# A smaller first batch, and its first expert phase run beside the routing of the last six tiles

## The reference

```python
h = tok(x, W, b); h = concatenate([cls_tok, h], axis=1)
h = h + attn(layernorm(h))                       # 12 heads; a neighbour filter on the scores before the softmax
# the experts, on y = layernorm(h):
logits_fk = (y @ W_fk + b_fk) @ normed(emb_fk).T   # 128 experts, first layer
logits_rk = (y @ W_rk + b_rk) @ normed(emb_rk).T   # 128 experts, second layer
w_fk = top4_of_softmax(logits_fk); w_rk = top4_of_softmax(logits_rk)
mid = sum_n w_fk[n] * (y   @ f_know[n])            # f_know: 128 matrices of 192 x 128
out = sum_n w_rk[n] * (mid @ r_know[n])            # r_know: 128 matrices of 128 x 192
h = h + out
```

## Time and profile before

| | us |
|---|---|
| runs (median of three) | 835.84, 830.92, 826.09 (830.92) |
| profiled execution | 832.31 |
| its span | 830.6 |
| groups 5 and 6 on PE | 240.9 to 280.5, 280.5 to 322.2 |
| last matmul of the attention groups | 346.6 |
| phase 0, first transpose to `experts_done[0]` | 408.3 to about 491 |
| phase 1, first transpose to last matmul | 491.5 to 577.6 |
| phase 2 | 629.0 to 698.9 |
| phase 3 | 713.1 to 775.6 |

### The profile page before, as it was taken

The page is one execution under the profiler, slowest core; times in us unless marked ns, Lnnn a source line. Parts: engine busy times, 40 slices in busy tenths (PEclk is TensorE's granted clock), DMA queues, the critical chain, the costliest instruction groups (busy, mean ns, idle before and its releaser), DMA issues.

```text
span 830.6 us, 16386 instructions
## 1 busy us (share of the span) xinstructions
PE 565.4 (68%) x5060; PEld 456.6 (55%) x5061; DVE 382.3 (46%) x1355; ACT 340.8 (41%) x738; POOL 403.8 (49%) x397
## 2 busy tenths in 40 slices
PE   6898998989999947516698859865018775777200
PEld 6686876868787836303578746654015453546100
DVE  2836678878676888998860001111111110133132
ACT  4337385564757425223255524432002553244100
POOL 2432260532514040767374027777667771576374
PEclk9689999999897968556699977988558998897755
DMA  5896769587840743395388747869996886588532
GB/s 138 315 364 275 262 239 386 206 346 279 325 170 21 156 98 77 106 284 139 107 270 238 203 119 202 234 187 293 309 291 187 266 264 185 169 242 255 171 99 69
DMA packets 151442, 177.44 MB, mean 214 GB/s; under 512 B 12777, under 2 KB 134930, under 8 KB 151378
## 3 DMA queue, kind: packets, MB, share of 16 engines
q1 hardware_dynamic: 138002, 149.20, 56.8%
q0 software_dynamic: 13376, 27.41, 11.6%
HBM read 76.55 MB, written 100.02 MB: 213 GB/s over the span
## 4 chain that ended last, share of the span: by engine, by line
PE 32%; DVE 19%; issue 12%; DMA 12%; POOL 11%; ACT 9%; SPq 4%; POOLq 0%; ACTq 0%; DVEq 0%
POOL gat L703 7%; PE bank L845 7%; DMA xs<-mid_dram 6%; PE bank L1133 4%; ACT qk_pad L1223 4%; PE bank L892 3%; POOL mid_dram L711 3%; PE bank L1107 3%; PE bank L1122 3%; DVE pick L1832 3%; DMA gat<-wide_dram,slots 3%; PE bank L1140 2%; PE bank L830 2%; SPq L494 2%; DVE smax L1609 2%
## 5 line engine op out<-in xcount | busy, mean ns | idle before, releaser
L703 POOL DMA_INDIRECT gat<-wide_dram,slots x152 | 145.7, 959 | 128.5 <-SPq L539 76.7
L1107 PE MATMUL bank<-ident,xs 128*96 128x128 f32 (+1 forms) x480 | 91.8, 305 | 62.7 <-DMA xs<-mid_dram 22.8
L1391 ACT ACTIVATE xsT<-bank 96x512 f32<-96x512 f32 (+1 forms) x160 | 76.4, 487 | 121.3 <-PE bank L1107 117.8
L1382 ACT ACTIVATE os<-bank 128x256 f32<-128x256 f32 (+1 forms) x160 | 70.1, 438 | 116.5 <-PE bank L1133 68.0
L647 POOL TENSOR_TENSOR qk_sum<-qk_pad 64x888 f32<-64x888 f32 x16 | 26.6, 1664 | 179.2 <-ACT qk_pad L1223 165.6
L1107 PEld LDWEIGHTS bank<-ident,xs 128*96 128x96 f32 (+1 forms) x480 | 59.4, 165 | 94.2 <-issue 47.9
L1879 DVE TENSOR_SCALAR acc<-gat,wts 128x128 f32<-128x128 f32 x19 | 5.6, 294 | 226.8 <-DMA gat<-wide_dram,slots 226.8
L690 POOL DMA_INDIRECT wide_dram<-x2b,slots x76 | 77.3, 1017 | 62.8 <-issue 58.0
L1133 PE MATMUL bank<-matrices,xsT 96*128 (+1 forms) x576 | 98.5, 310 | 1.9 <-ACT xsT L1391 1.8
L711 POOL DMA_INDIRECT mid_dram<-comb,slots x76 | 74.1, 975 | 27.3 <-issue 22.7
L1133 PEld LDWEIGHTS bank<-matrices,xsT 96*128 96x128 f32 (+1 forms) x576 | 80.8, 199 | 8.3 <-issue 5.4
(11 more groups left out here) (187 smaller groups left out, 990.8 us busy)
## 6 DMA issues: line engine op xcount, KB each, us to landing
wide_dram<-zeros SPq DMA_DIRECT2D x6, 5632.0 KB, 19.5
mid_dram<-zeros SPq DMA_DIRECT2D x8, 2816.0 KB, 25.7
xs<-wide_dram SPq DMA_DIRECT2D x80, 192.0 KB, 3.4
wide_dram<-os SPq DMA_DIRECT2D x80, 192.0 KB, 3.2
matrices<-in_L_ffn_f_know SPq DMA_DIRECT2D x8, 1536.0 KB, 15.3
matrices<-in_L_ffn_r_know SPq DMA_DIRECT2D x8, 1536.0 KB, 12.7
wide_dram<-os SPq DMA_DIRECT2D x80, 128.0 KB, 3.5
xs<-mid_dram SPq DMA_DIRECT2D x80, 128.0 KB, 3.6
```

The costliest lines, as they stand in the source:

```text
L703: pool.indirect_dma_start(gat[i][:, e, :], None, wide_dram[b], bass.IndirectOffsetOnAxis(ap=slots[:, t, k:k + 1], axis=0))\
L1107: last = pe.transpose(bank[r % 2][0:kp, c:c + ROWS], src, ident[:])
L1382: act.activation(os_[r][:, :, 0:width], bank[2 + r][:, 0:SB * width].rearrange("p (k w) -> p k w", w=width), ACT.Copy)\
L1391: act.activation(dst, src, ACT.Copy).then_inc(t_copied[ph], 1)
```

## The change

- `BATCHES` is cut at `READY[4]` = 9: batch 0 has 9 tiles and batch 1 has 10. `plan(0)` now falls in group 5 and not 6, and `SLOTTED` puts the slots of tiles 0 to 4 into group 6 and of tiles 5 to 8 into group 7. `ALL_STEPS` becomes 21. `rank` is int16 and lies elsewhere, and `xs` no longer shares its room with the routing tiles.
- Phase 0 starts behind `plan(0)` and the scatters of batch 0 alone. PE, ACT: its 16 fixed units and its first step of blocks run with the routing of the last six tiles (13 to 18) and `plan(1)` between them, in one order written by hand. It uses three result banks instead of four, others for the transposes, and no warm-up matmuls.
- The late chunks of `f_know` have a semaphore each, which PE waits for at units 8, 10, 12 and 14.
- All three late chunks of `r_know` are sent after `experts_done[1]`, ahead of the wait for batch 0's middle rows; before, one went ahead of `experts_done[1]` and two behind that wait.

```diff
-BATCHES = ((0, READY[5]), (READY[5], TTILES))
+BATCHES = ((0, READY[4]), (READY[4], TTILES))
-WARM = (12, 0, 24, 16)
+WARM = (0, 0, 24, 16)
+TURN_BANK = (6, 7)
+BESIDE_BANK = (2, 4, 5)
+BLOCK_BANK = ((0, 4, 5, 2), (2, 3, 4, 5), (2, 3, 4, 5), (2, 3, 4, 5))
+F_EARLY = 4
-SLOTTED = {7: list(range(BATCHES[0][1]))}
+SLOTTED = {6: list(range(5)), 7: list(range(5, BATCHES[0][1]))}
...
             sp.wait_ge(plan_ev[0], 4)
-            for t in range(*BATCHES[0]):
-                sp.wait_ge(scattered[t], 64)
-            sp.wait_ge(plan_ev[1], 4)
+            for n in range(PAIRS):
+                sp.wait_ge(scattered[n], PAIR_ROWS[n])
             for r in range(RING):
                 load_rows(0, 0, r)
             expert_rows(0, rows_of_second)
             expert_end(0)
             expert_rows(1, None)
-            load_r(EARLY, r_late[0])
             expert_end(1)
+            for n in range(EXPERTS // CHUNK - EARLY):
+                load_r(EARLY + n, r_late[n])
             mid_rows(0)
             for r in range(RING):
                 load_rows(2, 0, r)
-            for n in range(1, EXPERTS // CHUNK - EARLY):
-                load_r(EARLY + n, r_late[n])
...
+            def units(lo, hi):                      # on PE
+                for u in range(lo, hi):
+                    s, r = divmod(u, RING)
+                    turned_rows(0, *divmod(u + 1, RING))
+                    if u == 0:
+                        pe.wait_ge(f_early, 16 * F_EARLY)
+                    elif u % 2 == 0 and u >= 2 * F_EARLY:
+                        pe.wait_ge(f_late[u // 2 - F_EARLY], 16)
+                    first_products(0, s, r, bank[BESIDE_BANK[(u + 2) % 3]], 3)
+            def first_phase():                      # on PE
+                pe.wait_ge(plan_ev[0], 4)
+                used = steps_of(0)
+                turned_rows(0, 0, 0)
+                units(0, 2)
+                ranks_before(last_tiles[0])
+                units(2, 3)
+                ranks_after(last_tiles[0])
+                ranks_before(last_tiles[1])
...
+                for t in end_tiles:
+                    route_transpose(t)
+                units(5, 7)
+                for t in end_tiles:
+                    route_logits(t)
+                units(7, 10)
+                ranks_before(end_tiles[0])
+                units(10, 11)
+                ranks_after(end_tiles[0])
+                units(11, 12)
+                ranks_before(end_tiles[1])
...
+                units(14, 15)
+                ranks_after(end_tiles[2])
+                units(15, 16)
+                starts = block_starts(0, FIXED)
+                turned_rows(0, FIXED, 1)
+                products(0, FIXED, 0, starts, bank[BESIDE_BANK[(0 + HELD // ROWS // SB + 2) % 3]], 3)
+                plan(1, 0)
...
+                products(0, FIXED, 1, starts, bank[BESIDE_BANK[(1 + HELD // ROWS // SB + 2) % 3]], 3)
+                plan(1, 1)
...
+                products(0, FIXED, 2, starts, bank[BESIDE_BANK[(2 + HELD // ROWS // SB + 2) % 3]], 3)
+                plan(1, 2)
...
+            first_phase()
+            pe.wait_ge(plan_ev[1], 4)
+            experts(1)
```

More of the change, by code:

```diff
@@ new lines, in turned_rows @@
+            def turned_rows(ph, s, r):
+                layer = PHASES[ph][0]
+                kp, parts = ((DH, 2), (RANK, 1))[layer]
+                pe.wait_ge(xs_loaded[ph][r], 16 * (s + 1))
+                pe.wait_ge(t_copied[ph], s * RING + r + 1)
+                for k in range(SB):
+                    for j in range(parts):
+                        src = xs[r][:, k, j:D:2] if layer == 0 else xs[r][:, k, 0:RANK]
+                        c = k * 256 + j * ROWS
+                        last = pe.transpose(bank[TURN_BANK[r % 2]][0:kp, c:c + ROWS], src, ident[:])
+                last.then_inc(t_filled[ph], 1)
@@ new lines, in block_starts, with products @@
+            def block_starts(ph, s):
+                layer, b = PHASES[ph]
+                _, starts = nc.values_load_multi_w_load_instructions(
+                    owner[0:1, b, layer, bass.ds((s - FIXED) * BODY, BODY)], engines=[mybir.EngineType.PE],
+                    min_val=0, max_val=(EXPERTS - 1) * (256, D)[layer],
+                    skip_runtime_bounds_check_because="owner is clamped to the experts where it is computed")
+                return starts
+            def products(ph, s, r, starts, out_bank, depth):
+                layer = PHASES[ph][0]
+                kp, parts, width = ((DH, 2, RANK), (RANK, 1, D))[layer]
+                pe.wait_ge(t_copied[ph], s * RING + r + 3)
+                pe.wait_ge(y_copied[ph], s * RING + (RING + r + 1 - depth))
+                for k in range(SB):
+                    for j in range(parts):
+                        c = k * 256 + j * ROWS
+                        last = pe.matmul(
+                            out_bank[:, k * width:(k + 1) * width], xsT[r % 2][0:kp, c:c + ROWS],
+                            matrices[0:kp, bass.ds(starts[r * SB + k] + j * ROWS, width)],
+                            start=j == 0, stop=j == parts - 1)
+                last.then_inc(y_filled[ph], 1)
@@ new lines, in block_steps @@
+            def block_steps(ph, used, first, depth):
+                with pe.Fori(first, ALL_STEPS) as s, pe.If(s < used):
+                    starts = block_starts(ph, s)
+                    for r in range(RING):
+                        if r + 1 < RING:
+                            turned_rows(ph, s, r + 1)
+                        else:
+                            with pe.If(s + 1 < used):
+                                turned_rows(ph, s + 1, 0)
+                        products(ph, s, r, starts, bank[BLOCK_BANK[ph][r]], depth)
@@ L1396, in experts @@
-                for s in range(FIXED):
-                    step(s)
-                with act.Fori(FIXED, ALL_STEPS) as s, act.If(s < used):
-                    step(s)
+                if ph == 0:
+                    first_phase()
+                for s in range(FIXED if ph > 0 else 0):
+                    step(ph, s)
+                with act.Fori(FIXED + (ph == 0), ALL_STEPS) as s, act.If(s < used):
+                    step(ph, s)
                 if ph < 3:
@@ L1402, in experts @@
                     act.sem_inc(y_copied[ph + 1], RING)
+            act.wait_ge(plan_ev[0], 4)
+            experts(0)
             act.wait_ge(plan_ev[1], 4)
-            for ph in range(4):
+            for ph in range(1, 4):
                 experts(ph)
```

261 lines of the change are left out of this document (129 added, 132 removed).

## The result

The changed kernel took 851.16, 848.11, 856.48 and 858.78 us, a median of 853.82 us; the kernel before, on the same chip, 829.38. The ratio is **1.0283**, 95% interval 1.0186 to 1.0379: slower, as forecast, but by 24 us and not by 44; 853.8 lies at the lower edge of the range of 853 to 892. The profiled execution took 851.16 us, span 849.4.

What follows compares the result with a forecast made beforehand. A chain of waits was taken to bound the kernel, through DVE and PE, PE's phases and POOL's gathers and scatters. Its nine steps, traced in order, gave a span of 874.9 against 830.6 (+44.3), forecast 875 us, range 853 to 892.

Steps and rivals of the forecast that it cites:

- Step 3: Routing interleaved behind phase 0's rows on PE: 60 us from first row to plan, ends 50 and 70; plan(1) ends at 447.
- The sign and the chain: Slower, chance 0.90: late plan(1) delays batch 1's scatters, these phase 1; POOL then gaps between batches and releases phase 3.
- 5 phase 1: Phase 1 on PE: 86.1 us for nine steps plus a tenth of 13.8, ending at 610.4.
- 7 batch 1 on POOL: POOL waits for phase 1, then ten tiles at 10.4 us each, ending at 733.6 against 688.8 before.
- step 4: Batch 1's 40 scatters: 51.3 us, ending at 502.4; scatter and row load land in about 4 us each, phase 1 at 510.5.
- step 9: Tail behind the last gathers: 58.5 us, two tiles more, less 3 (0 to 8) for quieter DMA engines; span 874.9.
- step 6: Phase 1's stores: out at 629.6 instead of 601, with one r_know chunk fewer ahead (−3.9) and one iteration less (−0.7).
- Step 1: Front part: plan(0) in group 5 costs +8 (0 to 10), group 6 costs 0 (−2 to +6); f_know chunks go out at 356.7.
- The rival with the shared port pair: DVE and POOL block each other in groups 5 and 6: +9 us, 884; chance 0.07.
- Step 2: Phase 0's first rows, queued behind the f_know chunks: PE starts phase 0 at 387 (ends 373 and 398), 408.3 before.
- Phases that keep pace with POOL: Phase 1 and its stores fit POOL's 94 us for batch 0, no gap: 835, or 824 with early rows; chance 0.10.
- the scatters don't hold phase 1: Plan ends by 428, so phase 0's end and skipping decide phase 1's start at 492: −18, 857; chance 0.08.

Runs made afterwards that it cites:

- slots_late: The changed kernel with the slots of batch 0's nine tiles all made beside group 7's work: 848.46 us, ratio 1.0215 to the kernel before.
- beside_only: The changed kernel with the old split of 11 and 8 tiles, slots all in group 7, interleaving kept: 825.15 us, ratio 0.9905 to the kernel before.
- rf11_again: The changed kernel with the old 11/8 split and no interleaving (routing and second plan ahead of phase 0), timed a second time: 814.46 us, ratio 0.9807.
- beside_stores: beside_only with phase 0's last four stores issued ahead of the wait for batch 1's scatters: 824.1 us, ratio 0.9946 to the kernel before.
- route_first: The changed kernel, split 9/10, without the interleaving: routing of the last six tiles and second plan ahead of phase 0; 837.84 us, ratio 1.0082.
- split_only: The kernel before with only the 9/10 split, slots of five tiles in group 6, no interleaving: 836.89 us, ratio 1.0052.

## Where the prediction failed, and what of it held

**Step 3 was the mis-sized term, and it is the step that failed.** The chain was right, the size was not: the forecast had 44 us, the medians differ by 24 and the spans by 18.8. I gave the interleaving 60 us from the first row to the plan; it took 434.35 − 388.85 = 45.5, below my lower end of 50. By its parts: the 16 units ran at some 1.63 us and not at 1.82, 26 instead of 29; the slow start cost 2 us and not 8, since 392.60 is already fast; twelve rank groups followed one another 0.44 us apart, 5 instead of 9; the transposes and logits 5; the units of blocks with the plan's steps 6.7 (427.61 to 434.35) instead of 9, though three such units stand ahead of the plan's last part and not the two that I counted. The last 0.8 us are short waits. I had priced the slow start by phase 1 of the same trace, where six units were slow at a granted clock of 0.54, and the ranks partly by rows at half clock.

**The sign and the chain held.** Phase 1 waited for batch 1's scatters, these for the plan, and the plan for the units in front of it; POOL had a gap between the batches; phase 3 was released by POOL; 58.5 us followed the start of the last gathers. Undoing the interleaving took away 16 us, undoing the split 29. One link was missing: POOL's gathers of batch 0 did not start directly behind the last scatter but 9.7 us later, behind SP's stores, which cost nothing.

**The smaller terms**, predicted and measured:

| step | predicted | measured |
|---|---|---|
| 1 chunks sent | 356.7 | 357.6 |
| 2 phase 0 starts | 387 | 388.85 |
| 3 first row to plan | 60 | 45.5 |
| 4 forty scatters; last to phase 1's start | 51.3; 8.1 | 52.0; 4.0 |
| 5 phase 1 | 99.9 | 98.8 |
| 6 its stores to batch 1's gathers | 19.2 | 13.3 |
| 7 batch 1 on POOL | 104 | 103.5 |
| 8 last scatter to phase 3; to the gathers | 9.5; 76.3 | 8.1; 72.8 |
| 9 the start of the last gathers to the end | 55.5 | 58.5 |

Steps 3, 6 and the landing of step 4 make 24.5 of the 25.5 us by which the span was over-estimated; the others cancel. The 3 us that I took off in step 9 for quieter DMA engines did not come there. In step 4 I added a landing of the scatter to one of the rows and took 4 for each; together they took 4.0. In step 6 I had let the last three chunks' issue run 6.6 us past PE's last product (10.5 before, less 3.9 for one chunk); it ended with it, at 593.39 against 593.24, and only the skipping loop stood between it and the stores at 601.78.

**Step 1 came out within 1 us, and in part by luck.** I had +8 for the plan in group 5 and 0 for group 6. By the table of slots_late it was 11.4 and 2.6, and 1.5 behind group 7's first scores: 15.5 us. The groups ahead, where nothing is changed, were 6.5 us faster in this execution, and so the chunks left only 8.9 us later. The rival with the shared port pair wanted up to 9 us more in group 6 and did not come: POOL's arithmetic there (301.81 to 305.48) fell between the slots of two tiles. Step 2 came out right by its own mechanism, the rows behind the chunks: the scatters were over early (the last at 372.73, against 394.45 before), and the 5.6 us until the rows were sent and the 9.6 us that they took ate the gain.

**The rivals.** Phases that keep pace with POOL did not come, though the gap was 14 us and not 34. That the scatters don't hold phase 1 needed a plan by 428; it came at 434, and the bracket at 494.41 names the rows.

**What I had not seen** is why the two halves lose. The windows of PE's wait for rows and of phase 0, with the interleaving and without it, both at 11/8 (beside_only first, then rf11_again; the columns are those of the earlier trace rows):

```profile
337.80:389.40 51.60, 0.00 (x0) 0.00 (x0) 35.08 (x194) 0.38 (x1) 34.58 (x35) 0.50 0.79 206
389.40:477.80 88.40, 79.40 (x986) 68.21 (x986) 39.93 (x216) 57.00 (x146) 28.52 (x29) 0.96 0.65 185
```

```profile
345.00:398.70 53.70, 16.71 (x75) 9.86 (x74) 47.70 (x250) 13.59 (x52) 35.73 (x35) 0.56 0.76 202
398.70:475.40 76.70, 69.27 (x913) 60.17 (x912) 27.09 (x160) 45.33 (x95) 32.03 (x32) 0.97 0.76 216
```

PE waits over 50 us for the scatters of batch 0 in either kernel. Without the interleaving 16.7 us of routing lie in that wait, for nothing, though at a granted clock of 0.56. With it PE has no instruction there, and phase 0 is 11.7 us longer, 10.1 of them PE's own work. The 9 us by which beside_only starts phase 0 earlier are mostly its front part's: its chunks went out at 339.80, rf11_again's at 347.07. beside_stores, whose chunks went out at 347.93, starts phase 0 at 397.58, 1.2 us ahead of rf11_again, and phase 1 at 494.15, 10.4 us behind it, which is the whole loss. The interleaving moved work from a stretch in which PE waits to one in which it is the bound. With 9/10 it also makes the plan 30 us later, and the scatters become the wait.

The split's cost without the interleaving, rf11_again to route_first, is read from the starts: phase 1 at 483.80 and 484.46, phase 3's warm-up at 688.92 and 697.52 (+8.6, POOL's 14.6 us gap and ten tiles behind phase 1), the last gathers at 766.20 and 780.54 (+14.3, a tenth step), and tails of 48.1 and 58.3: 24.5 us in the spans. In split_only the same costs stood against a phase 1 that came 9.9 us earlier, and against late chunks that no longer waited: SP sent the last two at 596.04 and phase 2's warm-up began at 606.68, against 609.61 and 620.79 before. So the rest of the change, worth some 17 us at 11/8, is worth nothing at 9/10. Its largest part, 11 us, repaired the chunks' wait for batch 0's middle rows; the split alone ends this wait too, and then makes POOL's batch 1 the one that releases phase 3.

## What to carry to other kernels

Before work is interleaved into a phase, look at what the engine does in the stretch that the work leaves: if it waits there for something else, the work was free. Part a bundled change by a table of two by two before judging any piece: here one edit was worth 11 us beside one split and nothing beside the other, because the wait that it removed was there only with eleven tiles in batch 0, and with ten in batch 1 another engine released the next phase. Profile a kernel more than once before reading small differences of its stages: the part ahead of group 5 differed by up to 8 us between executions. When a chain is cut into batches, count the tiles that lie behind the last phase: nothing covered them here (10.4 us for two).

## What the runs showed of the hardware

**How long TensorE stays slow at the start of a phase varies.** Phase 1 began in the kernel before with six units whose 32 products took 1.93 us instead of 1.08 (20.8 us for seven units), with two such units in the change and with one in rf11_again, always behind an idle stretch (8.4, 23.2 and 8.4 us). The granted clock over those 20.8 us, and in the 12.7 us behind them:

```profile
491.50:512.30 20.80, 20.80 (x264) 14.90 (x267) 2.71 (x8) 7.32 (x15) 15.58 (x17) 0.54 0.61 161
512.30:525.00 12.70, 11.03 (x250) 8.52 (x249) 1.73 (x6) 6.24 (x14) 9.65 (x11) 1.00 0.81 224
```

In the change's 33.8 us without a matmul the granted clock was 0.50 (1.2 GHz), and over phase 0 it was 0.96:

```profile
355.00:388.80 33.80, 0.00 (x0) 0.00 (x0) 13.02 (x63) 0.32 (x1) 14.42 (x15) 0.50 1.03 264
388.85:471.30 82.45, 73.50 (x938) 63.53 (x938) 46.29 (x254) 54.03 (x141) 25.53 (x25) 0.96 0.63 176
```

The Trainium skill (TensorE: Matmul & The Clock Gate, Part 1: The HAM clock gate) says that the number of slow matmuls at a start differs between runs of the same kernel; these traces, though of different kernels, agree. One phase of one trace was no price for another here.

**Small DVE instructions waited out POOL's arithmetic.** DVE and then POOL in the change, in group 6:

```profile
302.05 1.64 DVE L1721 TENSOR_TENSOR h<-att,h_res 101x192 f32<-101x192 f32 x1
...
303.81 1.68 DVE L1862 SCALAR_TENSOR_TENSOR den<-zsum,s 128x4 f32<-128x4 f32 x1
```

```profile
301.81 1.67 POOL L646 TENSOR_TENSOR qk_sum<-qk_pad 64x888 f32<-64x888 f32 x1 [37.79 <-ACT qk_pad L1277]
303.56 1.92 POOL L648 TENSOR_TENSOR qk_pad<-qk_pad,qk_sum 64x888 f32<-64x888 f32 x1
```

`den` has four elements a partition and a median of 0.16 us over its twelve places; here it takes 1.68 us and ends at 305.49, as POOL's instruction ends at 305.48. By the rule of the Trainium skill (SBUF — State Buffer, SBUF: two separate sides), an exclusive lock on the shared port pair that makes a DVE instruction with two SBUF inputs wait for the end of a GpSimd one that reads SBUF and came first, this is what must happen, and the trace agrees. The slots' own write still took 0.17 us in each of its 19 places, none of them beside POOL's arithmetic in group 6.
